# Value projections tile by tile, an earlier input norm, later running sums and normed keys on VectorE in a one-core two-layer kernel

## What is computed

```python
xn = layernorm(x)
s = softmax_attention(xn)      # 16 heads of 64, causal, 256 tokens, Wq Wk Wv Wo
g = silu(moe_ffn(xn))          # top 1 of 8 experts, plus a shared expert (ws1, ws3, ws2)
x = x + s * g
xn = layernorm(x)
s = linear_attention(xn)       # 16 heads of 8, phi = elu + 1, running sums over the sequence
g = silu(local_stack(xn))      # two sublayers: token shift, qkv, l2norm of q and k, rotary,
                               # windowed attention (8 heads of 64), Wo, layernorm, GEGLU
x = x + s * g
```

## Time and profile before

| | us |
|---|---|
| median of 3 runs | 2111.61 |
| lowest, highest | 2111.47, 2113.14 |
| the profiled execution | 2113.86 |
| span of its instructions | 2112.1 |
| PE busy | 1783.7 (84%) |
| DVE, ACT, POOL busy | 1255.7, 1187.6, 895.2 |
| mean granted clock of PE | 0.922 of full |

### The profile page before, as it was taken

The page is one execution under the profiler, slowest core; times in us unless marked ns, Lnnn a source line. Parts: engine busy times, 40 slices in busy tenths (PEclk is TensorE's granted clock), DMA queues, the critical chain, the costliest instruction groups (busy, mean ns, idle before and its releaser), DMA issues.

```text
span 2112.1 us, 38035 instructions
## 1 busy us (share of the span) xinstructions
PE 1783.7 (84%) x12532; PEld 1147.1 (54%) x12532; DVE 1255.7 (59%) x4179; ACT 1187.6 (56%) x3527; POOL 895.2 (42%) x1025
## 2 busy tenths in 40 slices
PE   6679989997989889987989889987989798685876
PEld 4358754663565456654465456554565455363554
DVE  4434447556666556656766556656766656867653
ACT  2444547655656665666666565566566565553643
POOL 2633216523643245423553255414653255647510
PEclk9889999999999989999999999999999997787978
DMA  8146500000000000000000000000000000000000
GB/s 234 45 157 208 189 16 5 8 1 1 6 2 16 1 1 6 17 1 1 6 1 16 1 1 7 16 1 1 6 2 11 1 6 1 1 6 0 1 1 11
DMA packets 49725, 53.49 MB, mean 25 GB/s; under 512 B 6386, under 2 KB 42236, under 8 KB 49532
## 3 DMA queue, kind: packets, MB, share of 16 engines
q0 software_dynamic: 7808, 27.79, 4.0%
q1 hardware_dynamic: 41724, 23.26, 3.9%
HBM read 41.60 MB, written 9.44 MB: 24 GB/s over the span
## 4 chain that ended last, share of the span: by engine, by line
PE 46%; DVE 12%; issue 10%; ACT 7%; POOL 7%; DVEq 0%; ACTq 0%; POOLq 0%
PE ps L650 5%; PE ps L608 4%; PE ps L588 4%; PE ps L547 4%; PE ps L725 3%; PE ps L567 3%; PE ps L632 3%; PE ps L767 2%; PE ps L776 2%; PE ps L769 2%; PE ps L622 2%; POOL xn L308 2%; POOL big L1447 2%; DVE p L1033 2%; POOL big L1446 1%
## 5 line engine op out<-in xcount | busy, mean ns | idle before, releaser
L1333 POOL COPY rdx<-rden 128x256 f32<-128x256 f32 x256 | 99.5, 418 | 599.9 <-DVE rden L1050 574.9
L1033 DVE CUSTOM_DVE_ANT_0 p<-ps,mask 128x128 f32<-128x128 f32 (+1 forms) x512 | 152.2, 353 | 249.8 <-PE ps L580 215.3
L1033 DVE CUSTOM_DVE_ANT_0 p<-ps,mask,nrq 128x128 f32<-128x128 f32 x512 | 149.0, 347 | 204.1 <-PE ps L576 203.4
L588 PE MATMUL ps<-ident,p 128*128 128x128 f32 x1280 | 221.4, 297 | 26.8 <-ACT p L865 23.9
L865 ACT ACTIVATE p<-p,nmax 128x128 f32<-128x128 f32 (+1 forms) x512 | 226.4, 442 | 0.0
L725 PE MATMUL ps<-wqkv,hT 128*128 128x512 f32 x384 | 197.4, 623 | 27.9 <-ACT big L944 27.7
L864 ACT ACTIVATE p<-p,nmax 128x128 f32<-128x128 f32 x512 | 200.3, 391 | 34.5 <-DVE nmax L1033 34.0
L879 ACT ACTIVATE pt<-ps 128x384 f32<-128x384 f32 (+1 forms) x256 | 111.7, 436 | 185.2 <-PE ps L588 184.6
L588 PEld LDWEIGHTS ps<-ident,p 128*128 128x128 f32 x1280 | 143.8, 147 | 107.0 <-issue 89.2
L1446 POOL TENSOR_TENSOR big<-big,rots 128x512 f32<-128x512 f32 x64 | 99.6, 1556 | 206.0 <-ACT big L944 206.0
L557 PE MATMUL ps<-ident,big 128*128 128x128 f32 x512 | 90.9, 317 | 93.3 <-DVE big L1228 47.6
(11 more groups left out here) (251 smaller groups left out, 4207.7 us busy)
## 6 DMA issues: line engine op xcount, KB each, us to landing
slots_in<-xn SPq DMA_DIRECT2D x1, 2560.0 KB, 14.0
v<-slots_in SPq DMA_DIRECT2D x20, 128.0 KB, 4.6
slots_out<-v SPq DMA_DIRECT2D x20, 128.0 KB, 1.9
big<-in_x SPq DMA_DIRECT2D x4, 512.0 KB, 6.1
x<-in_x SPq DMA_DIRECT2D x8, 256.0 KB, 3.0
out_x<-x SPq DMA_DIRECT2D x8, 256.0 KB, 2.3
wqkv<-in_wqkv SPq DMA_DIRECT2D x2, 768.0 KB
xn<-in_x SPq DMA_DIRECT2D x6, 256.0 KB, 3.2
```

The costliest lines, as they stand in the source:

```text
L588: last = nc.tensor.transpose(bank[:, j * P:(j + 1) * P], c.p[:, u % 4, j * P:(j + 1) * P], c.ident[:, :])
L1033: last = V.tensor_tensor_reduce(out=c.p[:, u % 4, a:b], in0=bank[:, a:b], in1=mask, scale=scale, scalar=3e38, op0=ALU.add, op1=ALU.min, ac ...
```

## The change

1. `USES["v"]` is one place instead of four, and `values_of_tokens` takes one tile. Block 0 to 2 keep their ticks. For blocks 3 to 7, half 0 moves to 11 ticks before the block's first step (from 2 before), half 1 from 3 ticks before its own first step to 2 ticks before the block (two tiles) and 7 ticks after the block's start (two tiles).
2. For blocks 3 to 7, `xload`, `xn` and `xnT` come at 19, 18 and 15 ticks before the block's first step, from 5, 4 and 3. `ffn` of the block just finished then finds free ticks sooner: ticks 109 to 111 with `r` in 110 and `down0`, `comb` in 112 (from 114 to 117), and likewise in the other four periods.
3. Running sums: parts 2 and 3 of the first sequence come 2 ticks later, and `kv` of tiles 2 and 3 one tick later. The second sequence keeps its ticks.
4. `kn` makes all four tiles on DVE; POOL's half is gone.

Line numbers after the first loops are 3 to 4 higher in the changed kernel for the same code, 3 lower after POOL's `kn`.

```diff
-    "xnT": {"mm": 1}, "v": {"mm": 4}, ...
+    "xnT": {"mm": 1}, "v": {"mm": 1}, ...
-            for t, at in enumerate((-1, 0, 6, 7)):
+            for t, at in enumerate((-1, 0, 7, 8)):
                 self.put(l0 + at, "kv", b, t)
             for n in range(2 * LPARTS):
-                at = l0 + 1 + n + 4 * (n >= LPARTS)
+                at = l0 + 1 + n + 2 * (n >= 2) + 2 * (n >= LPARTS)
...
+        for b in range(2, BLOCKS):
+            f0 = self.first[(0, b, 0, 0)]
+            held.append((f0 - 5, f0 - 3) if b < XRING else (f0 - 19, f0 - 15))
...
-                self.put(f0 - 5, "xload", b)
-                self.put(f0 - 4, "xn", b)
-                self.put(f0 - 3, "xnT", b)
+                x0, x1 = held[b - 2]
+                self.put(x0, "xload", b)
+                self.put(x0 + 1, "xn", b)
+                self.put(x1, "xnT", b)
...
-            if b:
-                self.put(f0 - 2, "v", b, 0)
-            self.put(f1 - 3, "v", b, 1)
+            for t in range(TILES):
+                if b:
+                    self.put(f0 - (2 if b < XRING else 11), "v", b, 0, t)
+                self.put(f1 - 3 if b < XRING else f0 - 2 if t < 2 else f0 + 7, "v", b, 1, t)
...
     def kn(b, l):
         g = plan.turn[(b, l)]
         dve.wait_ge(c.r_ready, g + 1)
         dve.wait_ge(c.rot_ready, TILES * (g + 1))
-        for t in range(KN_VECTOR):
+        for t in range(TILES):
             k_over_norm(V, c, t).then_inc(c.kn_ready, 1)
...
-        for t in range(KN_VECTOR, TILES):
-            k_over_norm(G, c, t).then_inc(c.kn_ready, 1)
```

More of the change, by code:

```diff
@@ L44 @@
 RSQRT_MAGIC = 1597463007.0
-KN_VECTOR = 2
 class Common:
@@ L237, in lay_out @@
             self.put(l0 + 18, "s1", b)
-        held, shared = [(self.first[(0, b, 0, 0)] - 5, self.first[(0, b, 0, 0)] - 3) for b in range(2, BLOCKS)], {}
+        held, shared = [], {}
+        for b in range(2, BLOCKS):
+            f0 = self.first[(0, b, 0, 0)]
+            held.append((f0 - 5, f0 - 3) if b < XRING else (f0 - 19, f0 - 15))
         for b in range(BLOCKS):
@@ L242, in lay_out @@
             if b >= 2:
-                self.put(f0 - 5, "xload", b)
-                self.put(f0 - 4, "xn", b)
-                self.put(f0 - 3, "xnT", b)
-                assert f0 - 3 > shared[b - 2], b
-            if b:
-                self.put(f0 - 2, "v", b, 0)
-            self.put(f1 - 3, "v", b, 1)
+                x0, x1 = held[b - 2]
+                self.put(x0, "xload", b)
+                self.put(x0 + 1, "xn", b)
+                self.put(x1, "xnT", b)
+                assert x1 > shared[b - 2], b
+            for t in range(TILES):
+                if b:
+                    self.put(f0 - (2 if b < XRING else 11), "v", b, 0, t)
+                self.put(f1 - 3 if b < XRING else f0 - 2 if t < 2 else f0 + 7, "v", b, 1, t)
             for half in range(2):
@@ L460, in count_units @@
     for t in range(TILES):
-        mm.add(("v", 0, 0, t))
+        mm.add(("v", 0, 0, t, 0))
     mm.add(("q", 0))
@@ L533, in to_features, with values_of_tokens @@
         last.then_inc(c.mm_full, 1)
[L535 to L539, removed]
+    def values_of_tokens(b, half, t):
+        bank = mm_bank("v", b, half, t, 0)
+        MM(bank[:, :], c.xnT[:, b % 2, t * P:(t + 1) * P], c.wv[:, half * 512:(half + 1) * 512],
+           start=True, stop=True).then_inc(c.mm_full, 1)
     def produce(which, st):
@@ L595, in values @@
             if st.i == 0:
-                pe.wait_ge(c.mm_done, mm.done("qkv", st.b, st.part, END, 2) if st.kind else mm.done("v", st.b, st.part, END))
+                pe.wait_ge(c.mm_done, mm.done("qkv", st.b, st.part, END, 2) if st.kind else mm.done("v", st.b, st.part, END, 0))
         v = c.v1[:, plan.turn[(st.b, st.part)] % 2, :, :] if st.kind else c.v0[:, st.part, :, :]
@@ L638, in xnT, with v @@
         to_features(bank, c.xn0)
-    def v(b, half):
+    def v(b, half, t):
         pe.wait_ge(c.mm_done, mm.done("rT", b) if b < 2 else mm.done("xnT", b, 0))
-        values_of_tokens(b, half)
+        values_of_tokens(b, half, t)
     def wo(kind, b, part):
@@ L809, in tensor @@
     pe.wait_ge(c.wqk_loaded, 16 * 3)
-    values_of_tokens(0, 0)
+    for t in range(TILES):
+        values_of_tokens(0, 0, t)
     produce(0, plan.step(0))
@@ L847, in shifted, with values_of_tokens @@
         A(two(c.hT[HD:P, :])[:, :, 1:SEQ], two(bank[HD:P, :])[:, :, 0:SEQ - 1], ACT.Copy).then_inc(c.mm_done, 1)
-    def values_of_tokens(b, half):
-        for t in range(TILES):
-            evacuate(c.v0[:, half, t, :], "v", b, half, t)
+    def values_of_tokens(b, half, t):
+        evacuate(c.v0[:, half, t, :], "v", b, half, t, 0)
     def produce(which, st):
@@ L1461, in gpsimd @@
     stage = {"scatter": scatter, "wg": wg, "r": r, "xn": xn, "tables": tables, "lin": lin, "kv": kv, "qkv": qkv,
-             "kn": kn, "shift": shift, "cum": cum, "ln1n": ln1n}
+             "shift": shift, "cum": cum, "ln1n": ln1n}
     pool.memset(c.zero[:, 0, :], 0.0).then_inc(c.zero_ready, 1)
```

## The result

| | before | changed |
|---|---|---|
| median, us | 2112.3 (4 runs) | 2142.65 (4 runs) |
| lowest, highest | 2111.47, 2113.14 | 2140.04, 2143.68 |
| span of the profiled execution | 2112.1 | 2138.3 |

The ratio is 1.0142, with a 95% interval of 1.0124 to 1.0159. The forecast was 2101.1, and its range ended at 2126.

The account below looks back on a forecast made before the run. PE (TensorE), busy 84%, was taken to set the pace, so only its idle or low-clock time could be won. −3.0 a period, five times −15, plus 4.5 outside gave −10.5: median 2101.1 us, range 2066 to 2126.

Parts of the forecast that it names:

- a: Second norm's chain on VectorE: the running sums leave it, so its stretched instructions shorten, −1.9 us per period.
- b: Clock behind the wait of the second norm's transposes: the shorter wait spares half of 2.24, −1.1 us per period.
- c: PE's work around second norm's transposes: sums +1.0, two projections +1.85, four leaving tick 130 −3.69; together −0.8 us per period.
- d: PE newly waits before the second sequence's first running sum for kv of tile 3; with half a clock drop, +4.5 us.
- e: Earlier input norm: load and products cost nothing, its transposes at tick 102 add one copy, +0.6 us per period.
- f: Normed keys at tick 107 all on VectorE: −1.1, plus half a clock drop −1.1, together −2.2 us per period.
- g: Feed forward in ticks 109 to 111, half of v elsewhere: ticks 109 to 118 take 71.1 us, −2.1 per period.
- The first: More is won: the new wait before the second sequence's running sum vanishes in all seven places, −31, 2070 us; chance 0.17.
- The second: Slower: VectorE's serial chain at ticks 115 to 118 adds 5 us per period, 2126 us; chance 0.14.
- The third: GpSimd and VectorE exclude each other on SBUF while four kn tiles are made: +5.5 per period, 2129 us; chance 0.03.
- The fifth: The new wait is longer: GpSimd's copy 2 us later, each wait costs a whole drop, +22, 2123 us; chance 0.04.
- The fourth: No change: yT's shorter wait spares no clock drop and feed forward gives only 0.5 us; 2114.6 us; chance 0.14.

Follow-up runs that it names:

- e11: Changed kernel with the second sequence's running sums one tick later, kv untouched: 2114.33 us, ratio 0.9999.
- e1: Changed kernel with kv of tile 3 in the same tick as tile 2: 2101.24 us, ratio 0.9935.
- e2: Changed kernel with running sums and kv back at their old ticks (item 3 undone): 2097.65 us, ratio 0.9916.
- e12: Changed kernel with the second sequence's running sums and fin each one tick later: 2094.29 us, ratio 0.9906.
- e10: Changed kernel; second layer: kv of tiles 2, 3 together in blocks 0 to 5, old sums and kv places after; two value projections one tick sooner: 2083.59 us.
- e9: Changed kernel with fin, a block's last products on VectorE, one tick later: 2142.25 us, ratio 1.014.

## Why the forecast was wrong, point by point

Times per period, mean of four, from the start of one tick's logits to another's in the two traces.

| step | ticks | forecast | measured |
|---|---|---|---|
| a, b, c: the norm's chain, clock, PE's work behind `yT` | 119 to 126 | −0.2 | +0.8 |
| c: four projections leave tick 130 | 130 to 133 | −3.7 | −3.5 |
| d: the new wait | 127 to 129 | +4.5 | +6.8 |
| e: earlier input norm (with tick 134's clock) | 134 to 141 | +0.6 | +1.6 |
| f: `kn` | 142 to 144 | −2.2 | −0.5 |
| g: feed forward | 145 to 154 | −2.1 | −1.3 |
| sum | | −3.1 | +3.9 |

**d** was the right mechanism at the right place, and the first of the steps that failed, by size: 6.8 in place of 4.5, +2.3 in each of five periods, and 5.9 in block 0. The working took GpSimd's durations from a tick in which VectorE did nothing with two inputs, though `fin` stood in the very tick to which I moved the product, and it priced the clock at half a drop of 2.24 where each such wait cost 2.8. The upper bound of 5.6 was too low as well. In block 6 ticks 269 to 272 are 10.7 us longer, for which I had taken 4.5 of d. Not all of it is this wait: the wait of 5.81 with 2.8 for its clock is 8.6, and e11, in which the wait is gone from these ticks, takes 34.98 for them, 8.5 less.

**a** held, with −1.6 for −1.9. The chain has no stretched instruction any more, and PE waits 2.99 in place of 4.58:

```profile
860.46 0.17 DVE L288 TENSOR_SCALAR scratch<-scratch 128x4 int32<-128x4 int32 x1
...
863.90 1.08 PE L536 MATMUL ps<-ident,h 128*128 128x128 f32 x4 [2.99 <-DVE h L312]
864.78 1.17 PE L736 MATMUL ps<-big,tri 128*128 128x288 f32 x2
865.95 3.07 PE L541 MATMUL ps<-wv,xnT 128*128 128x512 f32 x4
```

**b** failed. The clock falls behind 2.99 us of waiting as behind 4.58: the transposes take 1.08 for four. What was then put behind the wait runs at half speed: the sum is 1.17 and not 0.5, the two projections 3.07 and not the 1.85 of **c**. So the saving of the wait was given back by the work that now stands behind it.

**e** held (0.5 at tick 138), but the clock fell at the next wait, tick 134, in all four periods, where before it did in two (that stretch took 54.6 to 54.8 us there with the fall and 52.4 without). That is the other 1.1.

**f** failed by its second term. `kn` now releases PE at 757.08, after a wait longer than before:

```profile
749.50 0.63 PE L560 MATMUL ps<-ident,big 128*128 128x128 f32 x4 [1.74 <-DVE big L1232]
...
757.08 1.94 PE L560 MATMUL ps<-ident,big 128*128 128x128 f32 x8 [4.49 <-DVE big L1323]
```

The first wait is 1.74 for a forecast of 1.8. From there to the second release are 7.58 us, before they were 8.45, so `kn` did win 0.9. Here the clock did come back: from the first release to PE's next wait (749.50 to 752.59) it was 1.00, where it was 0.50 before. But PE, at full clock, only stands 4.49 us instead of 2.82: the stretch is VectorE's (19.14 of 23.44 us busy), and a faster PE in it wins nothing. The half drop that I credited was time that was never PE's. In the mean of four periods ticks 142 to 144 won 0.5, so `kn` itself was over-sized too.

**g** held in kind, 72.56 us for the 71.1 expected, and −1.3 in the mean for −2.1.

**The rivals.** The first (no wait) is what e1, e2 and e12 made by an edit; it came to 2094 to 2101, not the 2070 that I had worked out, mainly since the terms around it were worth 3.2 us a period and not 7.5. The second (VectorE at ticks 115 to 118) didn't happen: PE waits 3.6 us at tick 116, and the half clock there lasts 10 us, in a stretch that is still shorter than before. The third names the right mechanism at the wrong place: ports don't meet at `kn`, they meet at `fin`. The fifth (0.04) is the nearest to what came, but only in its second half: each wait did cost a whole drop, while GpSimd's copy was not 2 us late. Its 2123 was 20 us short. The fourth, no change, didn't come, but of its two reasons the first did: `yT`'s shorter wait spared no drop.

The sum of all: d is some 17 us worse, 11.5 in the five periods, 1.4 in block 0 and 4.1 in block 6. The other terms fell short by 4.7 us a period in the four that are measured (3.1 + 4.5 forecast without d, 3.9 − 6.8 measured) and by 1.5 in the fifth, 20 together. That is 37 of the 41 us between 2101.1 and 2142.65; the rest lies at the start and the end, and I haven't divided it. By kind, most of it is the clock: d's drop cost 1.7 more than I took, b's credit of 1.1 and f's of 1.1 were worth nothing, and tick 134 added 1.1 in e. These are 5.0 of the 7.0 us that a period missed by. The step that failed is the price of the clock, in d first of all.

## What to carry to other kernels

When an instruction is moved into another tick, look at what every other engine does in that tick before taking its duration along: here both the moved products and the work beside them changed, 2.2 to 2.66 and 0.69 to 2.98 us. Work that fills a wait belongs ahead of the waiting instruction in the engine's order (0.7 us at the place in e10); behind it, it is added, here at the lower clock. A wait that one engine causes can hide a second one: taking one away (e9, e11) gives less than its price until the other goes too (e12). And a credit for PE's clock is only worth something where PE, and not the engine that it waits for, sets the length of the stretch.

## What the hardware showed

A shorter wait of TensorE spared the drop of the clock in some places and not in others. Behind waits of 4.58, 3.95, 3.18, 2.99 and 1.73 us the next transposes or sums ran at 1.2 GHz. Behind the 1.74 us at tick 107 of the changed kernel they ran at 2.4 GHz, where they had run at 1.2 behind 5.34 in the kernel before. So in these traces the length of the wait alone doesn't decide it. A tick with a wait of 3.95 us lost 6.7. VectorE's products with two inputs in SBUF took 2.60 and 2.98 us beside GpSimd's 128x1152 products, for 0.69 alone, while GpSimd's lost 0.3 to 0.4: the small instruction paid the length of the large one. It is not only products: an int32 instruction of the inverse root with one input, 128x64 (L289), took 2.48 us beside GpSimd's addition in e1, and 0.20 without.
